# Gated cross-attention and soft mixture-of-experts attention on one core: expert weights loaded, scaled and split at other places of the head

## The reference, cut to what matters

```python
x = x + tanh(g_xattn) * xattn(ctx, layernorm(x), Wk, Wq, Wv)
x = x + tanh(g_ffn) * ffn(layernorm(x), sim, gates, q_proj, k_proj, v_proj, o_proj)

def xattn(batch, latent, Wk, Wq, Wv):      # 77 keys for each of 128 queries
    w = softmax((latent @ Wq.T) @ (batch @ Wk.T).T / sqrt(128))
    return w @ (batch @ Wv.T)

def ffn(h, sim, gates, q_proj, ...):       # 16 experts, 64 sequences of 128 tokens
    logits = normalize(x) @ normalize(sim) - sigmoid(gates)
    w = softmax over the experts with logit > 0 (the best two where there is none)
    q, k, v = [sum_e w[:, e] * (x @ p[e]) for p in (q_proj, k_proj, v_proj)]
    o = softmax(q @ k.T / sqrt(128)) @ v
    return sum_e (w[:, e] * o) @ o_proj[e]
```

## Time and profile before

| | |
|---|---|
| median of 3 runs | 880.05 us (879.66 to 880.3) |
| profiled execution | 878.19 us, its span 876.4 us |
| PE busy | 822.3 us (94%), 4344 instructions |
| DVE busy | 618.1 us (71%) |
| ACT busy | 518.2 us (59%) |
| POOL busy | 550.7 us (63%) |
| DMA | 150.49 MB, mean 172 GB/s |
| chain that ended last | PE 80%, DVE 6%, ACT 5%, issue 4% |

### The profile page before, as it was taken

One profiled execution on the slowest core, in us unless ns is written; L12 is line 12 of the kernel. 1 busy time (PEld: TensorE's weight loads), 2 busy tenths in 40 slices (PEclk: granted clock), 3 DMA queues, 4 the chain that ended last, 5 costly groups with the idle time before them and its releaser, 6 DMA issues.

```text
span 876.4 us, 16223 instructions
## 1 busy us (share of the span) xinstructions
PE 822.3 (94%) x4344; PEld 458.2 (52%) x4344; DVE 618.1 (71%) x1575; ACT 518.2 (59%) x1148; POOL 550.7 (63%) x588
## 2 busy tenths in 40 slices
PE   4579999999999999999999999999999999999974
PEld 3445555555555555555555555555555555545431
DVE  3777577777686867768686776868677686876545
ACT  3555657565665756566575656657575565656353
POOL 2265567576685857567585756759475765857464
PEclk9999999999999999999999999999999999999999
DMA  8753655453654645364564536465463636546342
GB/s 223 193 193 106 192 176 189 139 200 130 219 160 166 209 156 191 111 227 151 186 210 153 192 108 218 145 205 191 152 212 111 226 111 210 185 182 217 93 159 72
DMA packets 58531, 150.49 MB, mean 172 GB/s; under 512 B 5568, under 2 KB 22144, under 8 KB 58496
## 3 DMA queue, kind: packets, MB, share of 16 engines
q1 hardware_dynamic: 57776, 150.00, 51.8%
q10 hardware_dynamic: 720, 0.08, 0.1%
HBM read 145.34 MB, written 4.72 MB: 171 GB/s over the span
## 4 chain that ended last, share of the span: by engine, by line
PE 80%; DVE 6%; ACT 5%; issue 4%; POOL 2%; DMA 1%; ACTq 1%; DVEq 0%; POOLq 0%
PE acc_v L893 17%; PE acc_k L893 17%; PE acc_q L893 16%; PE acc_o L909 16%; DVE zo_full L756 2%; ACT pc L550 2%; PE m L1032 2%; PE m L960 2%; PE m L931 2%; POOL stage L460 2%; PE oT_p L985 2%; PE m L1014 1%; PE m L923 1%; PE m L1001 1%; DVE zq_full L746 1%
## 5 line engine op out<-in xcount | busy, mean ns | idle before, releaser
L455 POOL TENSOR_TENSOR zq<-zq_full,zq 128x512 f16<-128x512 f32 x192 | 224.6, 1171 | 201.0 <-ACT zq L508 200.9
L460 POOL TENSOR_TENSOR stage<-zo_full,stage 128x512 f16<-128x512 f32 x208 | 239.4, 1160 | 69.7 <-ACT stage L516 69.7
L508 ACT ACTIVATE zq<-zq_full 128x512 f16<-128x512 f32 x256 | 161.1, 630 | 203.6 <-DVE zq_full L746 199.2
L909 PE MATMUL acc_o<-stage,w_hi 128*128 128x512 f16 x512 | 193.5, 381 | 10.3 <-POOL stage L460 7.3
L746 DVE TENSOR_TENSOR zq_full<-wq_bc,x2T_p 128x512 f32<-128x512 f32 x256 | 172.9, 677 | 35.1 <-ACT x2T_p L609 26.5
L893 PE MATMUL acc_q<-zq,w_hi 128*128 128x512 f16 x512 | 194.7, 380 | 0.0
L893 PE MATMUL acc_k<-zq,w_hi 128*128 128x512 f16 x512 | 194.5, 380 | 0.0
L893 PE MATMUL acc_v<-zq,w_hi 128*128 128x512 f16 x512 | 194.5, 380 | 0.0
L756 DVE TENSOR_TENSOR zo_full<-stage,oT_p 128x512 f32<-128x512 f32 x256 | 169.9, 677 | 6.5 <-PE oT_p L985 5.9
L516 ACT ACTIVATE stage<-zo_full 128x512 f16<-128x512 f32 x256 | 158.2, 629 | 25.7 <-DVE zo_full L756 25.1
L909 PE MATMUL acc_o<-stage,w_lo 128*128 128x512 f16 x256 | 97.5, 381 | 0.0
(11 more groups left out here) (141 smaller groups left out, 1067.6 us busy)
## 6 DMA issues: line engine op xcount, KB each, us to landing
wq_bc<-w_rows SPq DMA_DIRECT2D x128, 512.0 KB, 5.0
stage<-w_rows SPq DMA_DIRECT2D x128, 512.0 KB, 4.0
out_dram<-x_all SPq DMA_DIRECT2D x16, 256.0 KB, 4.3
ctx_g<-in_ctx_dram SPq DMA_DIRECT2D x16, 154.0 KB
x_all<-in_x_dram SPq DMA_DIRECT2D x2, 256.0 KB, 6.7
x_all<-in_x_dram SPq DMA_DIRECT2D x1, 512.0 KB, 9.2
w_rows<-wT SPq DMA_DIRECT2D x16, 32.0 KB, 3.2
wq_sb<-in_L_xattn_Wq_dram SPq DMA_DIRECT2D x1, 64.0 KB, 5.5
```

What stands on the lines that cost most here:

```text
L455: nc.gpsimd.tensor_tensor(zq[:, 1, e % Z_SLOTS, :], zq_full[:, e % F_SLOTS, :], zq[:, 0, e % Z_SLOTS, :], ALU.subtract).then_inc(zq_lo_poo ...
L460: nc.gpsimd.tensor_tensor(zo[:, 1, e % Z_SLOTS, :], zo_full[:, e % F_SLOTS, :], zo[:, 0, e % Z_SLOTS, :], ALU.subtract).then_inc(zo_lo_poo ...
L508: nc.scalar.activation(zq[:, 0, e % Z_SLOTS, :], zq_full[:, e % F_SLOTS, :], ACT.Copy).then_inc(zq_hi_done, 1)
L909: last = nc.tensor.matmul(acc[O][:], w[:, O, e, :], zo[:, half, e % Z_SLOTS, :], start=(e == 0 and n == 0), stop=(e == E - 1 and n == 2))
```

## The change

Four things, by engine.

**SP** waits for Wq, Wk and the five small loads before it issues the first projection; the order of the loads stays.

**The maxima** are shared in three turns (Q and K, then V, then O), each with its own two trips between TensorE and VectorE. Turn 0 stands in pass -2 (VectorE slot 11, TensorE after the transposes of slot 12), turn 1 in pass -1 (VectorE slot 0, TensorE after the transposes of x2 in slot 2), turn 2 in pass 0 (TensorE after the experts of slots 5 and 10, VectorE in slots 7 and 12). The reduction of V moves to slot 0 of pass -1, that of O to slot 1 of pass 0.

**The splitting**: w_hi of Q and K at (-2, 14), V at (-1, 2), O at (0, 13); w_lo of Q at (-2, 15), K and V at (-1, 9), O at (1, 1).

**The first group**: in pass -2 xn moves from slot 3 to 7 and xnT from 5 to 8, behind the transposes of the context; VectorE does the norm of sim and the statistics of group 1 right after the reduction of Q, ahead of its slots.

The diff, cut to its core:

```diff
--- before.py
+++ after.py
@@ -321,8 +324,11 @@
-        HIGH_AT = [(-1, 2), (-1, 4), (-1, 8), (0, 1)]
-        LOW_AT = [(-1, 7), (-1, 9), (-1, 10), (0, 3)]
+        HIGH_AT = [(-2, 14), (-2, 14), (-1, 2), (0, 13)]
+        LOW_AT = [(-2, 15), (-1, 9), (-1, 9), (1, 1)]
+
+        UP_TURNS = [1, 1, 2, 3]
+        TURNS = [slice(Q, V), slice(V, O), slice(O, O + 1)]
@@ -338,9 +344,12 @@
             sp.dma_start(wk_sb[:], Wk).then_inc(kq_in, 16)
+
+            sp.wait_ge(kq_in, 16 * 2)
+            sp.wait_ge(small_in, 16 * 5)
             for m, w in enumerate((q_proj, k_proj, v_proj, o_proj)):
                 sp.dma_start(stage[:, m], w.rearrange("e c h -> c e h")).then_inc(proj_in[m], 16)
-                if m == 0:
+                if m == Q:
                     load_x(1)
@@ -406,6 +415,7 @@
             nc.gpsimd.memset(w_new[:], 0.0)
+            nc.gpsimd.memset(wmax[:], 0.0)
@@ -499,7 +509,7 @@
             def weight_high(m):
-                act.wait_ge(prep_dve, 5)
+                act.wait_ge(up_done, UP_TURNS[m])
@@ -556,7 +567,7 @@
-                    if s == 3 and has(g1):
+                    if s == (7 if first else 3) and has(g1):
                         wait(act, rstd1_step, 3 * g1 + 3)
@@ -567,7 +578,7 @@
-                    if s == 5 and has(g1):
+                    if s == (8 if first else 5) and has(g1):
                         wait(act, xnT_ps, g1 + 1)
@@ -642,36 +654,45 @@
-            def setup_weights():
+            def setup_sims():
                 dve.wait_ge(nrm_root, 1)
...
+            def share_top(turn):
+
+                dve.wait_ge(wmax_ps, 2 * turn + 1)
+                nc.vector.tensor_reduce(wmax_t[:], acc[O][0:4, 0:P], AX_X, ALU.max).then_inc(prep_chain, 1)
+                dve.wait_ge(prep_chain, 5 * turn + 1)
+                nc.vector.tensor_scalar(wmax_d[:], ident[0:4, 0:4], wmax_t[:], None, ALU.mult).then_inc(prep_chain, 1)
+
+            def share_back(turn):
+
+                of, step, n = TURNS[turn], prep_chain, 5 * turn
+                dve.wait_ge(wmax_ps, 2 * turn + 2)
+                nc.vector.tensor_scalar(wmax_all[:, of], acc[O][:, P:P + 4][:, of], 2.0 ** -60, 2.0 ** 60, ALU.max,
                                         ALU.min).then_inc(step, 1)
...
+                dve.wait_ge(step, n + 5)
+                nc.vector.tensor_scalar(w_up[:, of], w_up[:, of], W_UP, None, ALU.mult).then_inc(up_done, 1)
...
@@ -779,6 +800,8 @@
                     setup()
                     weight_max(Q)
+                    setup_sims()
+                    first_stats(1)
@@ -814,13 +837,27 @@
                     if s == 9 and first:
                         weight_max(K)
-                    if s == 10 and has(g1 + 1):
+                    if s == 10 and has(g1 + 1) and not first:
                         first_stats(g1 + 1)
...
                     if s == 11 and first:
+                        share_top(0)
+                        share_back(0)
+                        setup_scores()
+                    if s == 0 and second:
                         weight_max(V)
+                        share_top(1)
+                        share_back(1)
+                    if isinstance(i, int) and i == 0:
+                        if s == 1:
+                            weight_max(O)
+                        if s == 7:
+                            share_top(2)
+                        if s == 12:
+                            share_back(2)
+                            setup_out()
@@ -847,17 +884,15 @@
-                    if s == 15 and first:
-                        weight_max(O)
-                        setup_weights()
@@ -871,20 +906,22 @@
-            def share_weight_max():
-                pe.wait_ge(wmax_done, 4)
-                pe.wait_ge(prep_dve, 3)
-                nc.tensor.transpose(acc[V][0:4, 0:P], wmax[:], ident[:]).then_inc(wmax_ps, 1)
-                pe.wait_ge(prep_chain, 4)
-                pe.wait_ge(wvT_done, 1)
-                nc.tensor.matmul(acc[K][:, 0:4], ones[0:4, :], wmax_d[:], start=True, stop=True).then_inc(wmax_ps, 1)
+            def share_top(turn):
+                pe.wait_ge(wmax_done, (2, 3, 4)[turn])
+                pe.wait_ge(prep_chain, 5 * turn)
+                nc.tensor.transpose(acc[O][0:4, 0:P], wmax[:], ident[:]).then_inc(wmax_ps, 1)
+
+            def share_back(turn):
+                pe.wait_ge(prep_chain, 5 * turn + 2)
+                nc.tensor.matmul(acc[O][:, P:P + 4], ones[0:4, :], wmax_d[:],
+                                 start=True, stop=True).then_inc(wmax_ps, 1)
@@ -902,6 +939,7 @@
                 if isinstance(g, int) and g == 0 and e == 0:
                     pe.wait_ge(lo_done, 4)
+                    pe.wait_ge(prep_chain, 15)
@@ -935,11 +973,15 @@
-                if isinstance(i, int) and i == -1:
-                    share_weight_max()
+                first = isinstance(i, int) and i == -2
                 for s in range(E):
                     if has(i):
                         experts(i, s)
+                        if isinstance(i, int) and i == 0:
+                            if s == 5:
+                                share_top(2)
+                            if s == 10:
+                                share_back(2)
@@ -966,12 +1008,15 @@
                         last.then_inc(x2T_ps, 1)
+                        if isinstance(i, int) and i == -1:
+                            share_top(1)
+                            share_back(1)
...
-                    if s == 5 and has(g1):
+                    if s == (8 if first else 5) and has(g1):
                         wait(pe, xn_done, g1 + 1)
@@ -1025,6 +1070,9 @@
                         last.then_inc(pxT_ps, 1)
+                        if first:
+                            share_top(0)
+                            share_back(0)
```

More of the change, by code:

```diff
@@ L186, in flamingo_gated_moe_attention @@
         nrm_root = sem("nrm_root")
+        nrm_step = sem("nrm_step")
+        up_done = sem("up_done")
+        out_prep = sem("out_prep")
         bn1_done = sem("bn1_done")
@@ L613, in body @@
                         nc.scalar.activation(pxT[:], m1[0:S, :], ACT.Copy).then_inc(pxT_sb, 1)
-                    if isinstance(i, int) and (i, s) in HIGH_AT:
-                        weight_high(HIGH_AT.index((i, s)))
+                    for m, at in enumerate(HIGH_AT):
+                        if isinstance(i, int) and (i, s) == at:
+                            weight_high(m)
             passes(act, body)
@@ L661, in setup_weights @@
                                         ALU.min).then_inc(step, 1)
-                dve.wait_ge(step, 5)
-                nc.vector.tensor_scalar(w_pow[:].bitcast(U32), wmax_all[:].bitcast(U32), 0x7F800000, None,
+                dve.wait_ge(step, n + 3)
+                nc.vector.tensor_scalar(w_pow[:, of].bitcast(U32), wmax_all[:, of].bitcast(U32), 0x7F800000, None,
                                         ALU.bitwise_and).then_inc(step, 1)
-                dve.wait_ge(step, 6)
-                nc.vector.reciprocal(w_up[:], w_pow[:]).then_inc(step, 1)
+                dve.wait_ge(step, n + 4)
@@ L671, in setup_weights @@
-                dve.wait_ge(step, 8)
-                nc.vector.tensor_scalar(w_up[:], w_up[:], W_UP, None, ALU.mult).then_inc(prep_dve, 1)
+                                        ALU.mult, ALU.mult).then_inc(out_prep, 1)
+                dve.wait_ge(out_prep, 1)
                 dve.wait_ge(tanh_done, 1)
-                nc.vector.tensor_scalar(out_scale[:], out_scale[:], tanh_f[:], None, ALU.mult).then_inc(prep_dve, 1)
+                nc.vector.tensor_scalar(out_scale[:], out_scale[:], tanh_f[:], None, ALU.mult).then_inc(out_prep, 1)
@@ L858, in body @@
                             zo_low(g, e)
-                    if isinstance(i, int) and (i, s) in LOW_AT:
-                        weight_low(LOW_AT.index((i, s)))
+                    for m, at in enumerate(LOW_AT):
+                        if isinstance(i, int) and (i, s) == at:
+                            weight_low(m)
             passes(dve, body, x_in)
@@ L885, in experts @@
                     pe.wait_ge(lo_done, 3)
-                    pe.wait_ge(wmax_ps, 2)
-                    pe.wait_ge(prep_chain, 5)
+                    pe.wait_ge(prep_dve, 3)
+                    pe.wait_ge(wvT_done, 1)
                 wait_zq_low(pe, i, s)
```

19 lines of the change are left out of this document (7 added, 12 removed).

## The result

The changed kernel took 883.92 us, the median of 4 runs (883.47 to 885.18), beside 880.17 for the kernel before, run with it. The ratio is 1.0045, with a 95% interval from 1.003 to 1.006, so the kernel is slower, by 3.75 us (0.4%). The forecast was +3.55. In a second group of runs the changed kernel had 883.35 (5 runs) beside 879.36: 1.0047 [1.0033, 1.006]. A ratio is estimated from all the executions of its group, so it can differ a little from the quotient of the medians; two executions among the experiments (1095.59 and 1452.08 us), at a much lower granted clock throughout, are left out.

What follows compares the result with a forecast made beforehand. The prediction saw a head in which TensorE mostly waits, then a stream of expert products bound by TensorE. Start 1.1, turn 2 0.3 and hole 2.15 add 3.55 to 880.05, giving 883.6 us; range 881.3 to 885.3.

Steps and rivals of the forecast that it cites:

- the start: Head: the first expert product comes at 55.0 instead of 53.88, +1.1 us.
- The hole (+2.15): Pass 1: w_lo of O delays zq_full of expert 6, and TensorE waits before the logit product, +2.15 us.
- The clock in the hole (8%): Rival, pass 1: TensorE's clock falls during its wait there, costing 1.7 us more; 885.3 us, chance 8%.
- the 7.5: Head: small loads landing before 7.5 us would show the forecast wrong; it took 8.4.
- so x2 on ScalarE comes at 30.0: Head: x1 at 25.1 puts x2 at 30.0 instead of 30.11, nothing won or lost.
- The steps behind x2: Head: turn 1 and w_hi of V ahead of xn of group 1 make all that follows 1.1 us later.
- the landing of q_proj takes the chain's place: Head: q_proj landing at 14.5 holds nmax_x to 18.65, so only 0.4 of TensorE's 2.6 us earlier scores arrives.
- the context's cover is thin: Head: group 1's context lands about 39.5, TensorE wants it at 39.6; a later landing is paid in full.
- Turn 2 (+0.3): Pass 0: sharing O's maximum adds two TensorE products, in slots 5 and 10, +0.3 us.
- the old place of w_lo of O: Pass 0, slot 3: w_lo of O was taken as hidden there, since that pass has no pc yet.
- The hidden hole (13%): Rival, pass 1: a wait TensorE has anyway hides the delay from w_lo of O; 881.4 us, chance 13%.
- VectorE's backlog (5%): Rival, head: VectorE's amount of work, not the loads, is the bound, so the kernel gets faster; 876.9 us, chance 5%.

Runs made afterwards that it cites:

- e1: Changed kernel with w_lo of O at slot 3 of pass 1 instead of slot 1; 882.02 us, ratio 1.0026.
- e7: Kernel before with only w_lo of O moved, from slot 3 of pass 0 to slot 1 of pass 1; 881.41 us, ratio 1.0022.
- e2: Changed kernel with w_lo of Q at slot 7 of pass -1 instead of slot 15 of pass -2; 884.4 us, ratio 1.005.
- e4: Changed kernel without SP's two waits before the projections; 883.74 us, ratio 1.0049.
- e8: Changed kernel reordered so the first group's chain precedes large work, K's reduction behind x1, turn 1 in TensorE's idle time; 875.55 us, ratio 0.9958.
- e5: Kernel before with SP's two waits alone added; 880.12 us, ratio 1.0005.
- e3: Changed kernel with w_lo of Q at slot 7 of pass -1 and w_lo of O at slot 3 of pass 1; 880.98 us, ratio 1.0009.

## Why the prediction was right, and where it was wrong

**Sign and size: right, but the closeness is luck.** Forecast +3.55, measured +3.75 and +3.99. The steps of the sum speak of the stream, and there the traces have 5.9. The 2.35 more are the start (1.27 above the forecast) and the clock's fall (1.7, at nothing in the sum), less 0.7 in pass 0. The two large errors point the same way. The time is near the forecast all the same because the changed kernel's medians lie 1.9 to 2.2 below its traces, which nothing here explains.

**The hole (+2.15): right.** 2.05, at the place and by the queue that the prediction read from the earlier trace rows; e1 takes it away, e7 makes it alone. It was the one large term, and it could be read before the run since each of its three steps had a row.

**The clock in the hole (8%): it happened** in all four traces of kernels with the hole and the changed head (after, twice, e2, e4), at 1.7, the price that the earlier trace rows gave. The forecast set it aside as the hole was shorter than the one of the earlier trace rows and stood between dense work. e7 has the same hole without the fall. For the traces the chance of 8% was too low; what decides it stays open.

**The start (+1.1): a mis-sized term, 2.37.** Up to x1 it went better than thought. The small loads landed at 7.35, not 8.4, which is earlier than the 7.5 that the prediction had named as a sign of being wrong. It had let them share the engines with the projections from 7 us on only. DMA share and GB/s, of before, then of after:

```profile
5.00:6.00 1.00, 0.00 (x0) 0.00 (x0) 0.87 (x4) 0.00 (x0) 0.00 (x0) 1.00 0.48 116
```

```profile
5.00:6.00 1.00, 0.00 (x0) 0.00 (x0) 0.85 (x5) 0.00 (x0) 0.00 (x0) 1.00 0.63 171
6.00:7.00 1.00, 0.00 (x0) 0.00 (x0) 0.32 (x4) 0.00 (x0) 0.33 (x2) 1.00 0.49 120
```

From 5 to 7 us the kernel before, with q_proj and x issued behind the small loads, moved less (116, and 72 in the earlier trace rows), so the large loads held the small ones up before 7 us already; how stays open. q_proj landed at 14.0, not 14.5, and kept only half of that gain: it was issued at 7.46, and its first traffic stands at 9.1, 1.6 later and not 1.1 (the issue itself lasts 0.88, that of w_rows in the earlier trace rows 0.55). So nmax_x stood at 18.14 for 18.65 and x1 at 24.61 for 25.1, 0.5 earlier. Then x2: 31.34 for 30.0. The step that failed is "so x2 on ScalarE comes at 30.0": it took the time from x1 to x2 over from the kernel before, and put w_lo of Q beside it as work of VectorE alone. Queued between x1 and x2 is the second norm on GpSimd, and w_lo held its first instruction for 2.05 - 0.23 = 1.8. -0.5 + 1.8 makes the 1.3 that were missing. All that follows is late by 1.3 to 1.5: the logit product 35.51 for 34.05, xn 38.3 for 37.0, the first zq_full 52.53 for 51.25. The steps behind x2, turn 1 and w_hi of V ahead of xn, were right: 1.14 against a forecast of 1.2 (30.11 to 30.0 at x2, and +1.1 at the start).

The kernel before had the row, which the prediction didn't look for: GpSimd in time, while w_lo of V runs from 47.83 to 50.15, where nobody waits for it:

```profile
48.20 2.03 POOL L425 TENSOR_SCALAR shift<-mv 128x4 f32<-128x4 f32 x1 [16.40 <-DVE mv L629]
```

Beside a reduction of the same size (e8, GpSimd while VectorE reduces K from 23.09 to 25.34) nothing is held:

```profile
23.45 0.23 POOL L450 TENSOR_SCALAR shift<-mv 128x4 f32<-128x4 f32 x1 [3.83 <-DVE mv L644]
```

w_lo reads two tiles in SBUF, the reduction one. Two more rows of the kernel before, right behind that w_lo, tell whether the two inputs matter or the length:

```profile
50.30 0.23 POOL L426 TENSOR_SCALAR rstd<-mv 128x4 f32<-128x4 f32 x1
...
51.72 0.54 POOL L430 TENSOR_TENSOR shift<-shift,rstd 128x4 f32<-128x4 f32 x1
```

The first runs beside zq_full (50.16 to 50.82), whose second input x2T_p lies in PSUM, and keeps its 0.23. The second takes 0.20 elsewhere and here 0.54, up to 52.26: beside it VectorE makes zq_low (L761) from 51.51 to 52.20, from two tiles in SBUF. The Trainium skill (SBUF — State Buffer, SBUF: two separate sides) states this as a rule: VectorE and GpSimd share a pair of ports; a VectorE instruction with two inputs in SBUF and a GpSimd instruction that reads SBUF exclude each other, and whichever starts second waits for the whole of the first. The traces agree: 27.20 + 2.32 is the end of w_lo at 29.52, and the GpSimd instruction, which started at 27.56, ends at 29.61.

**The load order inside the start.** The prediction said that the landing of q_proj takes the chain's place, and it did: e4 gives back 1.3 of start without the waits, e5 loses 0.8 with them alone. It said that the context's cover is thin, at 39.5 for 39.6. It landed at 40.0 to 40.2 (e2, e3) and was hidden in the changed kernel only since TensorE came to it (40.88) 1.3 later than forecast. The two errors hid each other: without the held instruction the context costs 0.5 (e2) to 1.0 (e3).

**Turn 2 (+0.3) and the old place of w_lo.** Its two products stand in the stream with 0.27 and 0.38. But pass 0 as a whole gave 0.4 back (start +2.37, offset 2.0). The prediction had the old place of w_lo of O, slot 3 of pass 0, as hidden; it wasn't quite. TensorE in the kernel before:

```profile
74.26 0.79 PE L1001 MATMUL m<-ctxT,m_kq 128*128 128x308 f32 x2 [0.48 <-ACT ctxT L580]
```

This wait is there in each of the three traces with w_lo of O in slot 3 of pass 0 (before, before again, e5) and in none without, e7 among them, where nothing else differs. Pass 0 gives back 0.8 in e7 and 0.3 to 0.4 in the kernels that have turn 2 as well; an estimate from the two for turn 2 is some 0.4, near the 0.3. w_hi of O and the memset cost nothing that shows.

**Rivals.** The hidden hole (13%) and VectorE's backlog (5%) are refuted by the 2.05 and by nmax_x at 18.14 right behind VectorE's own work. But the reading behind the second one, that the head has time to give, was true in another form: with nothing large ahead of the chain, e8 starts 4.1 earlier than the kernel before.

## What to carry to other kernels

When a large instruction is moved on one engine, look at who else works at its new time, also on engines that it has no semaphore with: VectorE's work with two inputs in SBUF holds GpSimd (2.05 for 0.23), and a chain that runs through a tiny GpSimd step pays for it in full. Put bulk work of a head (reductions, splits, shares) behind the small chain of its first tile, on each queue, and order the loads by who is waited for first; to delay large loads for small ones moves the wait to the last of the large ones. In a stream that one engine bounds, find each wait that a late instruction passes on through the queues, and price it with the clock's fall as well as without.

## What the runs showed of the hardware that I had not expected

- A GpSimd instruction of 0.23 took 2.05 (2.03 in the kernel before) beside w_lo, and 0.23 beside a tensor_reduce of the same 128x2048 or beside a zq_full with one input in PSUM.
- TensorE's clock fell to 1.2 GHz for 3.4 us behind a wait of 2.05 between dense products, in four traces of four with the changed head, and didn't in a fifth with the same wait. Behind a wait of 2.79 near the end of the kernel before it stayed at 2.4 GHz in one trace and fell in the other.
- The small loads landed 1.6 earlier (7.35 for 8.94) with no large load issued behind them, although with the large loads the engines moved less up to 7 us, 116 and 72 GB/s from 5 to 7 for 171 and 120.
- The granted clock of the profile can miss a low clock: up to 59.7 the first expert products of the changed kernel take 0.63 and follow each other at 0.43, beside 0.38 and 0.21 from then on, in stretches with 1.00; in e1 the same products, equally slow, stand beside 0.50. So the clock of a stretch is best checked against its products, as with the 9 in the changed kernel's stretch behind the hole and the 18 in e7's.
